# Attention with one core: where a head's last two v halves stand, and when its sums are drained

## The reference

```python
qkv = jnp.einsum('btd,de->bte', x, w_qkv) + b_qkv
q, k, v = jnp.split(qkv, 3, axis=-1)            # then 16 heads of 16
q = _rope(q); k = _rope(k)
attn = jnp.einsum('bhqd,bhkd->bhqk', q, k) / math.sqrt(HEAD_DIM)
attn = jax.nn.softmax(attn, axis=-1)
out = jnp.einsum('bhqk,bhkd->bhqd', attn, v)
...
x = _layernorm(x + (out @ w_out + b_out))
gate, up = x @ wg.T, x @ wu.T                   # wg = w_gate / 127, and so on
x = _layernorm(x + (silu(gate) * up) @ wd.T)
```

## Time and profile before

| | |
|---|---|
| median of 3 runs | 2866.97 us |
| the profiled execution | 2870.14 us |
| its span, first to last instruction | 2868.1 us |
| TensorE matmul busy | 2811.7 us (98%) |
| VectorE busy | 2702.9 us (94%) |
| ScalarE busy | 2591.9 us (90%), of it 4096 exponentials at 601 ns |
| GpSimd busy | 1416.7 us (49%) |
| TensorE's granted clock, mean | 0.989 of full speed |

### The profile page before, as it was taken

How to read it: one execution, slowest core, us unless ns; L and a number is a source line. 1 busy time by engine, 2 the same in 40 slices (tenths; PEclk the granted TensorE clock), 3 DMA queues, 4 the chain that set the end, 5 groups by cost and what they waited for, 6 DMA issues and landing times. The chain is left out here.

```text
span 2868.1 us, 70575 instructions
## 1 busy us (share of the span) xinstructions
PE 2811.7 (98%) x27022; PEld 862.5 (30%) x27022; DVE 2702.9 (94%) x3088; ACT 2591.9 (90%) x4778; POOL 1416.7 (49%) x4133
## 2 busy tenths in 40 slices
PE   8989999999999999999999999999999999999998
PEld 4531222222222222222222222222222222246665
DVE  7989999999999999999999999999999999947777
ACT  5756999999999999999999999999999999976555
POOL 7851444444444444444444444444444444436553
PEclk9978999999999999999999999999999999999999
DMA  5431111111111111111111111111111111233431
GB/s 194 142 116 28 36 35 36 35 36 35 35 35 35 34 35 36 35 36 36 35 35 35 36 35 35 35 35 36 35 35 36 35 35 35 70 90 92 118 96 38
DMA packets 121519, 146.56 MB, mean 51 GB/s; under 512 B 52832, under 2 KB 87520, under 8 KB 121180
## 3 DMA queue, kind: packets, MB, share of 16 engines
q1 hardware_dynamic: 120892, 142.02, 17.0%
q10 hardware_dynamic: 288, 0.01, 0.0%
HBM read 106.30 MB, written 35.13 MB: 49 GB/s over the span
## 5 line engine op out<-in xcount | busy, mean ns | idle before, releaser
L102 DVE TENSOR_REDUCE tile_max<-s_ps 128x1 f32<-128x1024 f32 (+1 forms) x2048 | 2282.4, 1185 | 8.8 <-PE s_ps L91 2.8
L1063 ACT ACTIVATE probs<-st_ps 128x512 f32<-128x512 f32 x4096 | 2202.2, 601 | 71.0 <-PE st_ps L942 41.1
L953 PE MATMUL o_ps<-probs,kept_v 128*17 128x256 f32 x16384 | 1283.1, 385 | 25.7 <-ACT sums L1032 25.7
L91 PE MATMUL s_ps<-k,q 64*128 64x512 f16 x4096 | 1266.2, 386 | 11.0 <-DVE tile_max L102 9.2
L942 PE MATMUL st_ps<-q,k 64*128 64x512 f16 x4096 | 1249.5, 382 | 1.1 <-ACT probs L1063 0.8
L1198 POOL TENSOR_TENSOR larger<-spared 128x256 f32<-128x256 f32 x1107 | 342.8, 310 | 675.6 <-ACT spared L1038 598.5
L953 PEld LDWEIGHTS o_ps<-probs,kept_v 128*17 128x17 f32 x16384 | 273.6, 95 | 852.2 <-ACT probs L1063 445.6
L942 PEld LDWEIGHTS st_ps<-q,k 64*128 64x128 f16 x4096 | 256.1, 94 | 902.0 <-ACT probs L1063 842.3
L1207 POOL TENSOR_TENSOR spared<-spared,larger 128x256 f32<-128x256 f32 x984 | 318.4, 324 | 81.9
L1200 POOL TENSOR_SCALAR larger<-larger 128x256 f32<-128x256 f32 x1107 | 261.4, 236 | 96.8
L91 PEld LDWEIGHTS s_ps<-k,q 64*128 64x128 f16 x4096 | 250.2, 94 | 50.4 <-DVE tile_max L102 46.5
(11 more groups left out here) (119 smaller groups left out, 1625.3 us busy)
## 6 DMA issues: line engine op xcount, KB each, us to landing
q<-q_parts SPq DMA_DIRECT2D x193, 128.0 KB
k<-k_parts SPq DMA_DIRECT2D x193, 128.0 KB
x_t<-in_x_t SPq DMA_DIRECT2D x16, 512.0 KB, 7.2
q_parts<-parts SPq DMA_DIRECT2D x32, 256.0 KB, 2.6
k_parts<-parts SPq DMA_DIRECT2D x32, 256.0 KB, 2.6
heads_out<-sums SPq DMA_DIRECT2D x256, 32.0 KB, 2.1
kept_v<-heads_out SPq DMA_DIRECT2D x16, 512.0 KB, 6.1
kept_v<-inverses_out SPq DMA_DIRECT2D x32, 256.0 KB
```

The source lines that it names most:

```text
L91: mm = pe.matmul(s["s_ps"][g % 2][:, j * BANK:(j + 1) * BANK], s["q"][h % 2][rows, r // KW * P:(r // KW + 1) * P], s["k"][h % 2][rows, at: ...
L102: dve.tensor_reduce(s["tile_max"][h % 2][:, r // KW, r % KW:r % KW + 1], s["s_ps"][g % 2][:, columns], AX.X, ALU.max).then_inc(s["s_read"], 1)
L953: mm = pe.matmul(o_ps[c * 32:c * 32 + VM, at:at + HALF], t["kept"][:, h, kt, :], probs[(h * KT + kt) % RING][:, c * BANK + at:c * BANK + a ...
L1063: act.activation(probs[(h * KT + kt) % RING][:, c * BANK:(c + 1) * BANK], st_ps[n % ST][:, :], ACT.Exp, scale=scale).then_inc(exp_done, 1)
```

## The change

`ODD_LAST` goes and `LAST_V = 1` comes. In the slots 1 and 2 of every head (`LAST_V` and the one behind it) the odd transposed score stands in front of the v half; in all other slots of the heads 0 to 62 it stays behind it. Slot 1 takes both halves of the last key tile, slot 2 has no v half. The drain stands behind exponential 3 instead of 4. The clear stands behind tile 16 instead of 18, and the addition to `b_out` stays.

```diff
-    ODD_LAST = range(EXPS // 2)
+    LAST_V = 1
...
-                    odd_last = h + 1 < HEADS and n in ODD_LAST
+                    odd_last = h + 1 < HEADS and n not in (LAST_V, LAST_V + 1)
                     if not odd_last:
                         scores_t(h, 2 * n + 1)
                     before, half = divmod(n - 3, 2)
                     if before >= 0:
                         times_v(h, before, half)
-                    elif h > 0:
+                    elif h > 0 and n <= LAST_V:
                         times_v(h - 1, KT + before, half)
+                        if n == LAST_V:
+                            times_v(h - 1, KT - 1, 1)
                     if odd_last:
                         scores_t(h, 2 * n + 1)
...
-                    if e == QC and h > 0:
+                    if e == QC - 1 and h > 0:
                         drain(h - 1)
...
             for g in range(EARLY, MAXES + LEAD):
                 maximum(g)
+                if g == MAXES // 2:
+                    clear()
                 if g == MAXES // 2 + 2:
-                    clear()
                     dve.wait_ge(bias_done, 1)
```

## The result

| | before | changed |
|---|---|---|
| median of 20 runs | 2867.61 us | 2873.77 us |
| ratio, 95% interval | | 1.002 (1.0014 to 1.0026) |
| profiled execution / span | 2870.1 / 2868.1 us | 2873.0 / 2871.1 us |

The account below looks back on a forecast made before the run. VectorE was taken to set the pace, TensorE's drain wait being worth only about 0.13 us a head. 8.5 + 0.3 + 0.1 - 0.6 = +8.3 us on 2866.97 gave 2875.3 us, own range 2873 to 2881, 8 in 10 from 2865 to 2886.

Parts of the forecast that it names:

- VectorE is the slower engine: In the heads, VectorE's maxima take 1.13 us against TensorE's 1.093 a slot; of TensorE's 0.47 drain wait only 0.13 counts.
- Slot 1's chain: TensorE, slot 1: lone score 0.05 us behind exponential 0, first v half 0.31 later, second 0.43 after that.
- the 0.31: TensorE: spacing from the last score to the v half behind it, 0.31 us.
- the rule of the Trainium skill: Both v halves use the same rows, so the second's loads would lie open: some 0.10 us more a head.
- Slot 2's maximum: VectorE, slot 2: the maximum starts at 957.28 instead of 956.90, leaving VectorE idle 0.38 us instead of 0.13.
- the 0.45 from a score to its maximum: VectorE: a maximum starts 0.45 us behind its second score.
- To slot 10: From slot 4 to the spared half: TensorE runs at VectorE's 1.13 us; slot 10's first score 0.16 late, spared copy 0.13.
- the +0.14 us a head: Net lengthening of each of heads 1 to 61, 8.5 us together; range 0.11 to 0.22 a head.
- Head 62: Head without a spared half in slot 10, so VectorE's 0.26 us lateness stays.
- The last head: Head 63, no s scores: its 0.21 us wait goes, but the next v product comes some 0.1 us later.
- The clear: Memsets moved two tiles sooner, into VectorE's 1.74 us wait for TensorE: -0.6 us, once.
- Head 0: First head: it drains nothing, so no term was given for it in the sum.

Follow-up runs that it names:

- the light kernels: The kernel before and the changed one, each with every maximum in the heads over 512 of 1024 columns: 2851.99 and 2823.85 us.
- the sum over eight kernels: VectorE's idle time at three places of head 20, summed for before, changed and follow-up kernels; the head less the sum is 35.51 or 35.52 us in each.
- the odd score alone: Kernel before with only the odd score moved in front of the v half in slots 1 and 2, halves and drain untouched: 2873.58 us, ratio 1.0016.

## Why the prediction was right

- *VectorE is the slower engine, and only its idle time counts.* Shown by the light kernels, 0.45 us a head won on TensorE alone against 0.09 lost with VectorE at full work, and by the sum over eight kernels.
- *Slot 1's chain.* The lone score, the 0.31, the halves 0.43 apart (1.06 for two, 0.63 for one, now in the stream) came as worked out. The loads of both halves all lie within 0.56 us, beside the matmuls of 1.06, though they use the same rows:

```profile
954.26 0.56 PEld L953 LDWEIGHTS o_ps<-probs,kept_v 128*17 128x17 f32 x16 [0.23 <-issue]
```

So the rule of the Trainium skill that weight loads overlap only across row groups (TensorE: Matmul & The Clock Gate, "The mechanism") doesn't price these halves: by it some 0.1 us more, an estimate from the mean load of 95 ns, would have stood between them. The same section also lets a load run ahead into a background weight buffer; whether that is the case here no run tells.

- *Slot 2's maximum* was forecast 2.63 us behind the head's first exponential (957.28 - 954.65) and starts at 2.60. The mis-sized step is the 0.45 from a score to its maximum: here it is 955.89 - 955.47 = 0.42. In the earlier trace rows the s score is issued behind its transposed partner, here in front of it. The light kernels, where maxima wait for scores, have 0.44 to 0.46 for the first and 0.41 for the second.
- *To slot 10.* The mis-sized term is the +0.14 us a head. Against the earlier trace rows, slot 10's first s score was forecast 0.16 us late and is 0.14 ((963.96 - 953.29) - (965.18 - 954.65)); the copy of the spared half was forecast 0.13 late and is 0.10 ((965.31 - 953.29) - (966.57 - 954.65)). The head is longer by about the same, 0.09. The 0.03 of the step before, a lead of the transposed scores of 0.04 and not 0.03, and a 0.13 that the prediction took as 0.14 make up the difference. 61 heads give some 5.5 us where 8.5 were forecast. The term lies just under the lower end that was given for it (0.11). The copy of the spared half in the changed kernel, then in the one before:

```profile
965.31 0.59 ACT L1040 COPY spared<-s_ps 128x512 f32<-128x512 f32 x1
```

```profile
966.57 0.59 ACT L1038 COPY spared<-s_ps 128x512 f32<-128x512 f32 x1
```

- *Head 62* was forecast 0.26 us longer and is longer by 0.22 (40.47 us against 40.25).
- *The last head* was forecast 0.1 us longer and is longer by 0.35: the v half of slot 3 starts 4.95 us behind the head's first exponential (2507.01), where it was 4.60 (2509.03 - 2504.43). Slot 3's odd score starts 0.54 us late, waiting for exponential 4, because the scores of slot 2 stand behind both halves and a projection. TensorE of the changed kernel there, to be set against the earlier trace rows:

```profile
2509.44 1.13 PE L585 MATMUL s_ps<-w_out,kept_v 128*128 128x256 f32 x4
2510.51 0.60 PE L942 MATMUL st_ps<-q,k 64*128 64x512 f16 x3
2511.65 0.39 PE L942 MATMUL st_ps<-q,k 64*128 64x512 f16 x1 [0.54 <-ACT probs L1065]
2511.96 0.41 PE L953 MATMUL o_ps<-probs,kept_v 128*17 128x256 f32 x4
```

- *The clear*: -0.6 forecast, -0.74 measured.
- *Head 0* was forecast unchanged. In these two profiles it isn't, for a reason told below. The two profiled spans differ by 3.0 us and not by 6.2 since in the one of before the work ahead of the changed code happened to take longer: the run of maxima ahead of the moved clear starts at 199.04 in it and at 195.94 in the one of after.
- *The closeness of the total is in part luck.* The heads were forecast 3 us too high; the last head, and in these profiles head 0, took 0.25 and 0.7 us more than forecast, which hides a part of it. 2873.77 us is only just inside the forecast's own 2873 to 2881, and the kernel before lay 0.6 us higher in its 20 runs than in the 3 that the forecast starts from.

## What to carry to other kernels

The idle time of an engine on the chain isn't what removing it gives. Ask what the engine behind it does meanwhile: here VectorE used TensorE's wait to work off its backlog, and only the 0.13 us in which it ran dry could be won there. When two engines run within a few per cent of each other, put long steps of the faster one where the slower one's queue is full, and count the starvation of the slower one at every place where the order is uneven; one such count, taken to all three places in a head, gave the 0.3% that the change missed. A backlog that is filled at one place can pay at another, so count over the whole period and not at one wait.

## What the runs showed of the hardware

TensorE's granted clock is 0.50 when the slots start. In the stretch before it has only s scores and waits for VectorE's maxima, as here in the kernel before; whether that is why the clock is low there no run tests:

```profile
205.63 0.61 PE L91 MATMUL s_ps<-k,q 64*128 64x512 f16 x1 [0.47 <-DVE tile_max L102]
```

The order of the code doesn't fix when the clock rises: TensorE's order in head 0, which has no v halves in its first three slots, is the same in all three kernels below. Stretches of before and of after around slot 0 of head 0 (whose first exponential starts near 234.5 and 230.7 us; the column in front of the last two is the granted clock, 0.50 being 1.2 GHz and 1.00 being 2.4):

```profile
238.00:240.00 2.00, 2.00 (x13) 0.29 (x12) 1.54 (x2) 0.65 (x2) 0.00 (x0) 0.50 0.13 51
240.00:242.00 2.00, 2.00 (x22) 0.40 (x20) 1.61 (x2) 1.55 (x4) 0.00 (x0) 0.83 0.13 53
```

```profile
236.00:238.00 2.00, 2.00 (x14) 0.28 (x12) 1.23 (x1) 1.13 (x3) 0.00 (x0) 0.50 0.13 53
238.00:240.00 2.00, 2.00 (x24) 0.41 (x22) 1.59 (x2) 1.72 (x4) 0.00 (x0) 0.88 0.12 51
```

In the kernel before it rises some 6 us behind slot 0, in the changed one some 8. With the odd score alone, whose head 0 starts near 234.6, it rises about 3 us behind slot 0:

```profile
236.00:238.00 2.00, 1.72 (x13) 0.42 (x15) 2.00 (x3) 1.89 (x5) 0.00 (x0) 0.67 0.13 53
238.00:240.00 2.00, 2.00 (x24) 0.51 (x21) 2.00 (x3) 1.52 (x3) 0.00 (x0) 1.00 0.13 51
```

Head 0 takes the longer the later that is: 36.37 us with the odd score alone, 37.43 in the kernel before, 38.09 in the changed one. The 0.7 us between the last two is as much as the clear is worth. A difference of that size has to be read between two marks of one stretch, not in totals.
